# Cross-attention and FP4 feed-forward on one core: loads ordered by first need, context split 96 and 96, setup of the weights moved into tile 0's slots, last two tiles reordered

## The reference

```python
h = layernorm(x)
q = h @ Wq                      # 256 -> 16 heads of 64
k, v = ctx @ Wk, ctx @ Wv       # 192 -> 16 heads of 64
attn = softmax(q k^T / 8)       # 154 context rows
x = x + (attn v) @ Wo + bo
g = layernorm(x)
xq = fp4(g)                     # blocks of 16: scale = max|.|/6, round to the FP4 grid
hid = silu(xq @ fp4(w_gate)^T) * (xq @ fp4(w_up)^T)     # 704 wide
x = x + fp4(hid) @ fp4(w_down)^T
```

## Time and profile before

| | |
|---|---|
| Three runs, us | 912.17, 912.39, 910.47; median 912.17 |
| The profiled execution, us | 915.48 |
| Its span, us | 913.4 |
| Its mean granted TensorE clock | 0.981 |
| Busy: PE / DVE / POOL / ACT, share of the span | 92% / 78% / 59% / 57% |
| Chain that ended last: PE / DVE / issue / ACT / POOL | 65% / 21% / 6% / 4% / 2% |

### The profile page before, as it was taken

How to read it: one execution, slowest core, us unless ns; L and a number is a source line. 1 busy time by engine, 2 the same in 40 slices (tenths; PEclk the granted TensorE clock), 3 DMA queues, 4 the chain that set the end, 5 groups by cost and what they waited for, 6 DMA issues and landing times.

```text
span 913.4 us, 21461 instructions
## 1 busy us (share of the span) xinstructions
PE 842.0 (92%) x6254; PEld 806.2 (88%) x6254; DVE 714.8 (78%) x2157; ACT 523.8 (57%) x1878; POOL 540.8 (59%) x810
## 2 busy tenths in 40 slices
PE   4786899999999999989999999989999999999984
PEld 4766889999988999989988999989988999999874
DVE  5659788878777888867878888876877888887786
ACT  4544565666665566646656565656665665566530
POOL 6438676764545666646553666665644566665643
PEclk9989999999999999999999999999999999999997
DMA  8101000001010000001010000000100000000000
GB/s 240 43 17 44 7 19 13 24 8 47 8 36 25 11 23 9 23 16 42 13 36 19 14 24 13 17 14 14 48 7 19 13 18 19 12 17 13 7 6 17
DMA packets 20151, 23.22 MB, mean 25 GB/s; under 512 B 2658, under 2 KB 18250, under 8 KB 20042
## 3 DMA queue, kind: packets, MB, share of 16 engines
q1 hardware_dynamic: 20042, 21.94, 8.0%
HBM read 17.74 MB, written 4.19 MB: 24 GB/s over the span
## 4 chain that ended last, share of the span: by engine, by line
PE 65%; DVE 21%; issue 6%; ACT 4%; POOL 2%; DVEq 0%; ACTq 0%; POOLq 0%
PE ps_q L1160 10%; PE ps_s L1202 8%; PE ps_g L1245 8%; PE ps_t L1212 6%; PE ps_o L1225 5%; PE ps_o L1227 5%; PE ps_o L1226 5%; PE ps_g L1123 3%; DVE pT_lo L737 3%; DVE negmax L884 3%; DVE scales L764 3%; PE ps_m L1259 3%; PE ps_m L1261 2%; PE ps_m L1260 2%; ACT probs L678 2%
## 5 line engine op out<-in xcount | busy, mean ns | idle before, releaser
L511 POOL TENSOR_TENSOR probs<-probs,rsum 128x308 f32<-128x308 f32 x256 | 180.4, 705 | 265.2 <-DVE rsum L848 257.3
L678 ACT ACTIVATE probs<-ps_s,negmax 128x154 f32<-128x154 f32 x512 | 194.8, 386 | 218.3 <-DVE negmax L884 217.0
L884 DVE TENSOR_REDUCE negmax<-ps_s 128x2 f32<-128x308 f32 x256 | 121.1, 473 | 91.2 <-PE ps_s L1202 90.7
L1225 PE MATMUL ps_o<-B_sb,pT_lo 128*128 128x256 f32 x640 | 180.9, 283 | 0.9 <-DVE x_both L939 0.6
L1227 PE MATMUL ps_o<-B_sb,pT_hi 128*128 128x256 f32 x640 | 180.7, 282 | 0.0
L1226 PE MATMUL ps_o<-B_sb,pT_hi 128*128 128x256 f32 x640 | 180.4, 282 | 0.0
L737 DVE TENSOR_TENSOR pT_lo<-ps_t,pT_hi 128x256 fp32r<-128x256 f32 (+1 forms) x256 | 122.8, 480 | 34.0 <-ACT pT_hi L572 33.6
L1212 PE MATMUL ps_t<-ident,probs 128*128 128x128 f32 x640 | 113.8, 276 | 26.2 <-DVE pT_lo L737 23.8
L1245 PE MATMUL ps_g<-WGU,xqT_hi 128*128 128x352 f32 x504 | 131.8, 343 | 2.2 <-DVE B_sb L737 1.9
L1225 PEld LDWEIGHTS ps_o<-B_sb,pT_lo 128*128 128x128 f32 x640 | 121.0, 189 | 1.4 <-issue 0.8
L1227 PEld LDWEIGHTS ps_o<-B_sb,pT_hi 128*128 128x128 f32 x640 | 121.5, 190 | 0.0
(11 more groups left out here) (224 smaller groups left out, 2221.2 us busy)
## 6 DMA issues: line engine op xcount, KB each, us to landing
xa<-in_x_dram SPq DMA_DIRECT2D x33, 128.0 KB, 2.1
xr<-in_x_dram SPq DMA_DIRECT2D x32, 128.0 KB, 2.0
out_dram<-y_xn SPq DMA_DIRECT2D x30, 128.0 KB, 1.7
W_sb<-in_L_xattn_Wk_dram SPq DMA_DIRECT2D x4, 512.0 KB, 3.5
W_sb<-in_L_xattn_Wv_dram SPq DMA_DIRECT2D x3, 512.0 KB, 3.7
probs<-in_L_xattn_Wq_dram SPq DMA_DIRECT2D x2, 512.0 KB, 8.5
Wo_sb<-in_L_xattn_Wo_dram SPq DMA_DIRECT2D x1, 1024.0 KB, 9.6
VT<-in_L_ffn_w_down_dram SPq DMA_DIRECT2D x2, 352.0 KB, 3.4
```

What stands on the lines that cost most here:

```text
L511: pool.tensor_tensor(unit, unit, rsum[:, 2 * u:2 * u + 2].unsqueeze(2) .to_broadcast([P, 2, M]), ALU.mult).then_inc(norm_p, 1)
L678: ins = act.activation(probs[:, h, 0:M], ps_s[k % 2][:, s * M:(s + 1) * M], ACT.Exp, bias=negmax[:, h:h + 1], accum_out=sums[:, h:h + 1])
L884: dve.tensor_reduce(negmax[:, 2 * k:2 * k + 2], ps_s[k % 2][:, 0:UM].rearrange("p (h m) -> p h m", h=2), AX_X, ALU.max, negate=True).then_ ...
L1225: pe.matmul(ps_o[:, 0:C], lo[:, j, :], w[:, 0:C], start=first, stop=False)
```

## The change

Seven things change.

- **Loads.** SP issues x (two tiles), context rows 0 to 255, columns 0 to 255 of Wk, the rest of Wk, chunk 0, the other context rows, chunk 1, the first residual rows. After the first x transposes: two x tiles. After K 0 and K 1: the first half of Wv; after K 3: its second half, then Wo, chunk 2, bo. Wq comes in four chunks of 256 KB, issued by ACT on its own queue as its first instructions.
- **Context.** Its 192 columns are cut into 96 and 96 (`CH`). `W_sb` holds both halves, `Wkv_sb` and the zeroing are gone; `project` still makes four matmuls. A context tile is copied by one ACT instruction instead of three. In the later batches `load_w` brings 768 KB instead of 512.
- **Order of the start.** PE first makes 12 matmuls on the identity whose result nothing reads (`warm`), then two context tiles, K 0, 4 more such matmuls, then the x transposes. ACT, DVE and POOL follow that order; POOL zeroes K_hi and K_lo behind the first and second layernorm scale.
- **Slot 0.** K 1, K 2 and K 3 stand there, in banks "1", "t" (ps_t) and "o" (ps_o), and the other three context tiles, whose copies ACT makes in slot 1.
- **FFN weights.** Chunk 0 goes into slots 0 to 4; `RAW_AT` and `TURN_AT` change as shown.
- **The end, DVE.** The add of tile R = 29 and S's `hidden_lo` come ahead of T's last quarter; `hidden_part_lo(0)` comes ahead of `hidden_part(2)`.
- **The end, PE.** 8 and 16 matmuls whose result nothing reads (`busy`); T's down product is cut in two, the first third ahead of the transposes of parts 1 and 2.

```diff
-        W_sb = sb("W_sb", [P, INNER])
-        Wkv_sb = sb("Wkv_sb", [P, INNER])
+        W_sb = sb("W_sb", [CH, 2, INNER])
         Wo_sb = sb("Wo_sb", [P, PAIRS, C])
         Wq_sb = [sb(f"Wq_{n}", [P, KT, INNER], F32R) for n in ("hi", "lo")]
-        ctxT = sb("ctxT", [P, 3, NB * M])
+        ctxT = sb("ctxT", [CH, 2, NB * M])
...
-        BANKS = {"q": ps_q, "0": ps_g[0], "1": ps_g[1]}
-        FIRST_K = "01"
+        BANKS = {"q": ps_q, "0": ps_g[0], "1": ps_g[1], "t": ps_t, "o": ps_o}
+        FIRST_K = "0"
...
-            "start": {0: [("K", 2, "0"), ("K", 3, "1")], 1: [("V", 0, "0"), ("V", 1, "1")],
+            "start": {0: [("K", 1, "1"), ("K", 2, "t"), ("K", 3, "o")], 1: [("V", 0, "0"), ("V", 1, "1")],
...
-        RAW_AT = [None, 0, 2, 4, 6, 8, 11, 14]
-        TURN_AT = [1, 3, 5, 7, 9, 12, 14, 15, 18, 19]
+        RAW_AT = [0, 1, 3, 5, 7, 10, 11, 14]
+        TURN_AT = [3, 4, 7, 8, 10, 13, 14, 15, 18, 19]
...
+                sp.dma_start(W_sb[:, :, :], w.rearrange("(k p) n -> p k n", p=CH)).then_inc(ld_w, 16)
+
+            def load_w_cols(w, cols, done):
+                sp.dma_start(W_sb[:, :, cols], w[:, cols].rearrange("(k p) n -> p k n", p=CH)).then_inc(done, 16)
...
+            sp.dma_start(ctx_raw[:, 0:2, :], ctx_rows[0:2 * P, :].rearrange("(r p) c -> p r c", p=P)).then_inc(ld_ctx, 16)
+            load_w_cols(Wk, slice(0, 2 * P), ld_wk)
+            load_w_cols(Wk, slice(2 * P, INNER), ld_w)
             load_raw(0)
-            load_w(Wk)
-            for half, w in enumerate((Wk, Wv)):
-                sp.dma_start(Wkv_sb[half * D:(half + 1) * D, :], w[P:CC, :]).then_inc(ld_wkv, 16)
-            for n in range(2):
-                cols = slice(n * INNER // 2, (n + 1) * INNER // 2)
-                sp.dma_start(Wq_raw[:, :, cols], Wq[:, cols].rearrange("(k p) n -> p k n", p=P)).then_inc(ld_wq[n], 16)
+            sp.dma_start(ctx_raw[:, 2:full, :], ctx_rows[2 * P:full * P, :].rearrange("(r p) c -> p r c", p=P))\
+              .then_inc(ld_rest, 16)
+            sp.dma_start(ctx_raw[0:NB * M - full * P, full, :], ctx_rows[full * P:, :]).then_inc(ld_rest, 16)
             load_raw(1)
+            load_xr(0, bass.ts(0, P))
             sp.wait_ge(xT_mm, 1)
             load_xa(0, bass.ts(2, P))
             load_xa(1, bass.ts(3, P))
+            sp.wait_ge(k_mm, 2)
+            load_w_cols(Wv, slice(0, INNER // 2), ld_wv)
+            sp.wait_ge(k_mm, KV)
+            load_w_cols(Wv, slice(INNER // 2, INNER), ld_w)
             sp.dma_start(Wo_sb[:, :, :], Wo.rearrange("(q p) n -> p q n", p=P)).then_inc(ld_wo, 16)
...
-            pool.memset(K_sb[0][:, :, :].bitcast(F32), 0.0).then_inc(kpad_p, 1)
...
-            pool.memset(K_sb[1][:, :, :].bitcast(F32), 0.0).then_inc(kpad_p, 1)
+                pool.memset(K_sb[n][:, :, :].bitcast(F32), 0.0).then_inc(kpad_p, 1)
...
-            round_chunk(0)
...
+                act.activation(ctxT[:, :, cols], ctx_bank(r)[0:CH, :].rearrange("p (k n) -> p k n", k=2)[:, :, 0:rows],
+                               ACT.Copy).then_inc(pre_ev, 1)
...
+            for i in range(4):
+                cols = slice(i * 2 * P, (i + 1) * 2 * P)
+                act.dma_start(Wq_raw[:, :, cols], Wq[:, cols].rearrange("(k p) n -> p k n", p=P)).then_inc(ld_wq[i], 16)
+            layer_norm1_out(0, 0)
             for r in range(2):
+                act.wait_ge(pre_mm, r + 1)
                 context(r)
+            wq_hi_part(0)
+            layer_norm1_out(1, 1)
+            take_hi(("K", 0, FIRST_K[0]), 0)
             hi_part(xT_all(0), parts(ps_m, 4), (xT_mm, 1), xT_hi)
...
+                    if isinstance(t, int) and t == 0 and k == 1:
+                        act.wait_ge(pre_mm, CTX_T)
+                        for r in range(2, CTX_T):
+                            context(r)
...
-            chunk_scales(0)
-            chunk_divide(0)
+            wq_lo_part(0)
+            take_lo(("K", 0, FIRST_K[0]), 0)
             lo_part(xT_all(1), parts(ps_m, 4), xT_all(0), (xT_hi, 1), xT_lo)
-            take_lo(("K", 0, FIRST_K[0]), 0)
-            wq_lo_part(0)
-            take_lo(("K", 1, FIRST_K[1]), 0)
...
-                gate_by_up(T, 3, ehT, ps_gT[3])
-                largest_of(T, 3, ehT, hriT, am_v)
                 dve.wait_ge(d_mm, R + 1)
                 dve.wait_ge(y_a, R + 1)
                 dve.tensor_tensor(y[R % 2], y[R % 2], ps_m[:, 0:C], ALU.add).then_inc(y_v, 1)
-                hidden_part(2)
                 for r in range(2):
                     hidden_lo(S, r)
-                for i in range(3):
+                gate_by_up(T, 3, ehT, ps_gT[3])
+                largest_of(T, 3, ehT, hriT, am_v)
+                hidden_part_lo(0)
+                hidden_part(2)
+                for i in range(1, 3):
                     hidden_part_lo(i)
                 add_y(S, ps_m)
                 add_y(T, ps_s[1])
...
-            def project(ps, w, half, i, b, done):
+            def project(ps, w, i, b, done):
                 for n in range(2):
                     u = 2 * i + n
-                    cols = slice(u * P, (u + 1) * P)
-                    pe.matmul(ps[:, n * M:(n + 1) * M], w[:, cols], ctxT[:, 0, bass.ts(b, M)], start=True, stop=False)
-                    ins = pe.matmul(ps[:, n * M:(n + 1) * M], Wkv_sb[:, cols], ctxT[:, 1 + half, bass.ts(b, M)],
-                                    start=False, stop=True)
+                    for half in range(2):
+                        ins = pe.matmul(ps[:, n * M:(n + 1) * M], w[:, half, u * P:(u + 1) * P], ctxT[:, half, bass.ts(b, M)],
+                                        start=(half == 0), stop=(half == 1))
...
+            warm(12)
+            pe.wait_ge(ld_ctx, 16)
+            context_transposes(range(2))
+            pe.wait_ge(pre_ev, 2)
+            make(("K", 0, FIRST_K[0]), 0)
+            warm(4)
             pe.wait_ge(xln1_a, 2)
             m_free(None, (xT_lo, 1))
             both_transposes(ps_m)
...
+                    if isinstance(t, int) and t == 0 and k == 0:
+                        pe.wait_ge(ld_rest, 32)
+                        pe.wait_ge(k_lo, 1)
+                        m_free(None, (pre_ev, CTX_T))
+                        context_transposes(range(2, CTX_T))
...
+                busy(ps_m, 8)
...
+                pe.wait_ge(xqT_lo, T + 1)
+                part_transposes(0)
+                pe.wait_ge(h_v, Q * T + 2)
+                busy(ps_s[1], 16)
                 m_free(None, (y_v, S + 1))
                 pe.wait_ge(hqT_lo, 2 * S + 2)
                 down_terms(ps_m, *hqT, range(FT)).then_inc(d_mm, 1)
-                pe.wait_ge(h_v, Q * T + 2)
-                for i in range(3):
+                pe.wait_ge(hT_lo, 1)
+                down_terms(ps_s[1], *hqTT, range(2))
+                for i in range(1, 3):
+                    pe.wait_ge(h_v, Q * T + 2 * i - 1)
+                    part_transposes(i)
+                for i in range(1, 3):
                     pe.wait_ge(hT_lo, i + 1)
                     ins = down_terms(ps_s[1], *hqTT, range(2 * i, 2 * i + 2))
```

More of the change, by code:

```diff
@@ L794, in layer_norm1 @@
                 stats(xa[par][:, :], st1, mv1, rs1, (ld_xa[par], 16 * pairs), ln1_v, 3 * n)
-            for half in range(2):
-                h = slice(D - D * half, P - D * half)
-                dve.memset(ctxT[h, 1 + half, :], 0.0).then_inc(cpad_v, 1)
             def wq_lo_part(i):
@@ L1164, in _, with context_transposes, warm @@
             pe.wait_ge(ident_p, 2)
-            def context_transposes():
-                for r in range(CTX_T):
+            def context_transposes(tiles):
+                for r in tiles:
                     rows = min(P, NB * M - r * P)
                     for k in range(2):
-                        ins = pe.transpose(ctx_bank(r)[:, k * P:k * P + rows], ctx_raw[0:rows, r, k * P:(k + 1) * P],
+                        ins = pe.transpose(ctx_bank(r)[0:CH, k * P:k * P + rows], ctx_raw[0:rows, r, k * CH:(k + 1) * CH],
                                            ident[0:rows, 0:rows])
                     ins.then_inc(pre_mm, 1)
+            def warm(n):
+                for _ in range(n):
+                    pe.matmul(ps_q[:, 0:P], ident[:, :], ident[:, :], start=True, stop=True)
+            warm(12)
[4 more added lines that the diff above has]
+            warm(4)
             pe.wait_ge(xln1_a, 2)
@@ L1209, in turn_probs @@
                     pe.wait_ge(pT_lo, PAIRS * t + u)
+                else:
+                    free("t")
                 for j in range(blocks(u)):
@@ L1262, in down_terms, with busy @@
                 return ins
+            def busy(ps, n):
+                for _ in range(n):
+                    pe.matmul(ps[:, 0:C], Wq_sb[0][:, 0, 0:P], Wq_sb[0][:, 0, 0:C], start=True, stop=True)
             def step(pair, par, own=True, before=True, gate=True, down=True, out_=True, ahead=True, queries=True,
```

79 lines of the change are left out of this document (28 added, 51 removed).

## The result

The changed kernel takes 915.13 us (median of 8 runs, 914.07 to 917.34), the kernel before 911.94 beside it; the ratio is 1.0038 [1.0025, 1.005]. The change costs 3.2 us by the medians and 3.5 by the ratio (912 times 0.0038), where 8.0 us of gain were forecast. The two profiled executions are equally long: 915.17 us after, and 915.48 before, which stood 3.3 us above the median of the three runs shown with it.

The account below looks back on a forecast made before the run. From 140 to 160 us PE itself is the bound, so time could come only from the start and end: 5.4 + 2.6 = 8.0 us off the 912.17 us median, giving 904.2, range 899.5 to 909.5 (about 0.85).

Parts of the forecast that it names:

- The start's first scores: Slot 0: first scores start at 16.5 us (16.0 to 17.4) against 22.08, 5.6 us earlier.
- lead of 4.5 at slot 1: Slot 1: scores start at 23.5 us instead of 27.98, within 22.3 to 26.7 depending on PE's clock.
- They add 0.3: Slot 2: bias lands at 30.2, PE's probability transposes start at 31.6, costing 0.3 us; slot 3 starts at 34.9.
- Its own sign: Slot 2: the forecast is wrong if POOL's bias sum L532 ends after 33 us.
- the bias comes late: Rival, slot 2: bo lands at 33.5, PE's transposes start at 35.0, 3.5 us saved, 908.7 us; chance 0.13.
- Slower: Rival, slots 2 and 3: bias wait to 38 costs 7.8 us, half rate 3.5 more; 915.5 us; chance 0.05.
- Slots 3 to 6: Chunk transposes give back 0.9, leaving 3.0 us lead at slot 6; slot 6 takes 5.6 to 8.1, not 10.66.
- I take 1.5 lost: Slots 8 to 16: chunk 5's rounding on POOL moves right ahead of chunk 6's, losing 1.5 us.
- bound of 3.7: Slots 8 to 16: most that POOL's rounding of chunk 5 could cost, if slots 10 and 11 get no quicker.
- If slots 10 and 11 get quicker by as much: Slots 10 and 11: the condition under which chunk 5's later rounding on POOL loses nothing.
- The end: Last tiles: S's product starts about 902.8, last add at 908.2 instead of 910.82; 2.6 us saved, between 0.9 and 3.3.
- The bound of 1 us on Wq's queue: Start: Wq's loads on ACT's queue beside SP's cost nothing, at most 1 us, covered by POOL's memset.

Follow-up runs that it names:

- e6: e3 without the dummy matmuls at the start, warm(12) and warm(4); 908.72 us, 0.9965 of the kernel before.
- e1: The changed kernel with bo loaded ahead of the wait for the first x transposes, not behind Wo and chunk 2; 910.76 us, 0.9987 of the kernel before.
- e3: The changed kernel with bo loaded early and chunk 5 scaled, rounded and transposed one slot earlier; 909.33 us, 0.9955 of the kernel before.
- e4: The kernel before with only the new end (order and 24 dummy matmuls), nothing of the new start; 908.6 us, 0.9957 of the kernel before.
- e5: e4 with chunk 2 taken one slot earlier, so slot 5 has no chunk's transposes; 906.61 us, 0.9945 of the kernel before.
- e12: e8 with chunks 0 to 2 transposed in slots 2, 3 and 4, and chunks 3 to 5 as in the kernel before; 907.01 us, ratio 0.9952.
- e15: The same kernel as e4, measured again in another set on a different chip; 909.53 us, 0.9983 of the kernel before.
- e11: The changed kernel with the end of the kernel before, so the new start alone; 918.76 us, 1.0075 of the kernel before.
- e8: e3 with the four Wq transfers issued by SP behind the rest of Wk, not by ACT; 906.93 us, 0.995 of the kernel before.
- e14: The same kernel as e8, measured again in another set; 908.86 us, 0.9973 of the kernel before.

## Why the prediction was wrong

The time lies 10.9 us above the forecast of 904.2. The parts of the sum, one by one:

**The start's first scores** were right in kind: 17.42 us where 16.5 or, at half rate, 17.4 was said. Slot 1 was foreseen at 22.3 to 26.7 (its upper terms add up to 27.1) with 23.5 taken; it was 26.25, the end of the range, because the three K products ran at half rate, 2.25 us each. e6 shows that the dummies change nothing there. Of the lead of 4.5 at slot 1 only 1.7 was there.

**"They add 0.3"**, for the wait for the bias in slot 2, is the step that failed first. Its own sign came, L532's sum (L531 after the change) ending after 33, at 34.4. By e1 the late bias cost 4.7 us in all. The step had two parts. The landing was put at 30.2 with the issue at 22.8 (22.8, 5.1 and 2.1 add up to 30.0); the issue came at 27.85, since K 3 at half rate held SP's queue to about 26, and the landing at 33.6. The rival "the bias comes late" had this landing, to 0.1 us, by luck: Wo was issued 3.8 us later than it took, at 26.25, and the bias was there 7.3 us after that and not 11.1. It still gave 908.7, since it priced the wait by one consumer, PE's transposes. The second consumer, POOL's layernorm scale, ACT's output and the query behind it on ACT's queue, was not looked for. It moved PE's next work from 35.6 to 37.73 and left PE at the lower clock for A 0 and C 0, 1.6 us more. The lead of 0.8 which that rival kept at slot 3 was in truth a lag of 3.6. "Slower" gave 915.5, nearly the time measured, and that too is luck: its wait to 38 did not come, and the chunks' slots took the rest.

With the bias early, slot 3 starts at 35.11 in e1, close to the 34.9 of the forecast, but at 38.20 in e3, which has the same steps up to there. At slot 6, 0.0 to 1.2 us of the forecast lead of 3.0 are left. So the wait was not all that was wrong in slots 0 to 3: the K products were taken near full rate, and chunk 1's division, 3.8 us beside POOL's rounding in e1, is no term of the sum.

**Slots 3 to 6.** Slots 3 to 5 gave back 0.5 us more (0.9 forecast). Slot 6 takes 5.0 us where 5.6 to 8.1 were forecast, 5.7 less than in the trace of before and 4.3 less than in e4's. Its mechanism was right, and the experiments bear it out (e5).

**"I take 1.5 lost", slots 8 to 16,** was mis-sized beyond its bound of 3.7, and is the second step that failed. The lead went from +1.5 at slot 7 to -4.1 at slot 15, 5.6 us. Of this chunk 5 a slot earlier regains 2.2 to 2.5 by the traces, and the old slots for chunks 3 to 5 all the rest (e12). The bound counted POOL's rounding alone. DVE's division of chunk 5 together with chunk 6's scales ahead of the add that PE needs, a wait of 2.60 us (0.6 before), was not in it. Nor was chunk 6's division, which takes 3.9 us beside POOL's rounding (1.9 before), nor the lower clock from 84 to 100 us that followed the waits. "If slots 10 and 11 get quicker by as much" did not come.

**The end** was foreseen to save 2.6, at a start of S's product at 902.8 and with it an end at full rate. Measured: 1.5, 3.9 (e15, e4) and 3.4 (e11), and 1.4 to 1.5 in the traces (after, e4, e15). The size was right within that spread. The start of S's product was right too: counted from the last slot's maxima, it would stand at 902.65 on the time scale of before. The mechanism was half right, since the first half of that product is still at half rate, and by the traces the dummies cost 0.9 us.

**Shared transfer engines.** The bound of 1 us on Wq's queue is not shown to have held: slot 0 starts 1.05 us earlier in e8 than in e3, but 0.35 later in e14, and two pairs within sets differ by 1.6 and 1.8 us in time. The Trainium skill, "DMA: Bandwidth & Descriptors", "Issuing engines are not separate DMA queues", says that all queues share the same engines. The trace agrees: 7.2 us to land for 192 KB with Wq beside it, 3.4 without.

Summed up by the first scores against the trace of before: 4.7 us won at slot 0, 2.9 lost in slot 0, 2.0 won in slot 1, 7.4 lost in slot 2 (with the bias mended, 4.7 of this come back for good), 0.5 lost in slots 3 to 5, 5.7 won in slot 6, 5.6 lost in slots 7 to 14. That is 4.1 us of lag at slot 15, and the end gives 1.5 back: 2.6 slower, where the medians say 3.2. The new start alone costs 6.8 by time (e11). With bias and chunks mended (e12) it is worth no more than e5, which moves one chunk and leaves the start as it was: leads of 4.1 and 4.7 us at slot 16.

## What to carry to other kernels

When a transfer is moved back, list everything behind its first consumer on that consumer's queue and follow each to the next engine. The wait here stood in one instruction of POOL, and it was the scale behind it that held ACT, DVE and PE. A step that is moved one slot meets the next step's work on every engine it uses, so ask for a slot table of each engine and not of the busiest one. In that table look for large steps of DVE and POOL side by side, since a division on DVE took up to two and a half times as long there.

A single trace of the kernel before may be one of its slowest executions: compare stretches whose input is the same, and take sizes from runs of one set.
